# One projection a step in the last head group, and the map combination ahead of the maxima

## What is computed

```python
xn = _layernorm(x, axis=-1)
qkv = xn @ Wqkv_w.T + Wqkv_b                  # 16 query, 8 key heads of 128, values of 4 groups of 256
s = einsum('bqhd,bkhd->bhqk', q, k) * D ** -0.5
p1, p2 = softmax(causal(s)) of the even and of the odd heads
p = p1 - lam * p2
o = einsum('bhqk,bkhe->bqhe', p, v)
o = o * rsqrt(mean(o * o) + EPS) * subln_w * (1.0 - LAMBDA_INIT)
s = o @ out_w.T + out_b
g = silu(quant_dequant_mxfp4(xn) @ quant_dequant_mxfp4(weight).T + bias)
x = x + s * g
```

## Time and profile before

| what | value |
|---|---|
| runs | 1603.66, 1607.04 and 1606.81 us, median 1606.81 us |
| the profiled execution | 1607.1 us |
| its span in the trace | 1605.3 us |
| TensorE busy | 1486.7 us, 93% of the span |
| VectorE busy | 1133.6 us, 71% |
| ScalarE busy | 876.8 us, 55% |
| GpSimd busy | 857.5 us, 53% |

### The profile page before, as it was taken

How to read it: one execution, slowest core, us unless ns; L and a number is a source line. 1 busy time by engine, 2 the same in 40 slices (tenths; PEclk the granted TensorE clock), 3 DMA queues, 4 the chain that set the end, 5 groups by cost and what they waited for, 6 DMA issues and landing times.

```text
span 1605.3 us, 27534 instructions
## 1 busy us (share of the span) xinstructions
PE 1486.7 (93%) x8982; PEld 864.8 (54%) x8982; DVE 1133.6 (71%) x2654; ACT 876.8 (55%) x2474; POOL 857.5 (53%) x1587
## 2 busy tenths in 40 slices
PE   5777879999999989999999999999999998999978
PEld 2444445556555556455565565556564555555644
DVE  5888877667775777757776677757777477775761
ACT  5666765366634666346653566336663466535650
POOL 2566546555465544655455554655546554554543
PEclk9989899999999999999999999999999999999989
DMA  8245453334423453235433335234441344333333
GB/s 262 62 87 132 89 91 65 91 81 74 88 56 89 84 87 76 48 95 84 91 64 91 81 64 96 65 86 83 91 79 43 96 85 90 63 70 76 65 65 73
DMA packets 382496, 134.76 MB, mean 84 GB/s; under 512 B 361872, under 2 KB 365968, under 8 KB 382352
## 3 DMA queue, kind: packets, MB, share of 16 engines
q1 hardware_dynamic: 382352, 132.99, 39.7%
HBM read 35.93 MB, written 8.39 MB: 28 GB/s over the span
## 4 chain that ended last, share of the span: by engine, by line
PE 52%; DVE 16%; ACT 11%; POOL 9%; issue 7%; DMA 4%; SPq 1%; ACTq 0%; POOLq 0%; DVEq 0%
PE ps L544 15%; PE ps L546 14%; PE ps L545 14%; ACT pp L713 4%; DVE ps L1011 3%; DVE qkv L976 3%; PE ps L611 3%; PE ps L613 3%; PE ps L612 3%; ACT ph L722 2%; DMA pT<-ph 2%; ACT qkv L690 2%; DVE ph L1023 2%; POOL qkv L1210 1%; ACT on L735 1%
## 5 line engine op out<-in xcount | busy, mean ns | idle before, releaser
L713 ACT ACTIVATE pp<-ps,row 128x384 f32<-128x384 f32 (+3 forms) x512 | 267.6, 523 | 262.9 <-DVE row L1011 262.7
L1226 POOL TENSOR_TENSOR row<-row,small 128x1 f32<-128x1 f32 x256 | 150.9, 590 | 431.5 <-ACT pp L713 431.5
L544 PE MATMUL ps<-xT,wqkv 128*128 128x512 f16 x768 | 295.6, 385 | 18.8 <-DVE qkv L976 7.8
L1011 DVE CUSTOM_DVE_ANT_0 ps<-ps,mask,ssc 128x384 f32<-128x384 f32 (+3 forms) x512 | 280.0, 552 | 37.5 <-PE ps L613 36.0
L545 PE MATMUL ps<-xT,wqkv 128*128 128x512 f16 x768 | 295.4, 385 | 0.0
L546 PE MATMUL ps<-xT,wqkv 128*128 128x512 f16 x768 | 295.4, 385 | 0.0
L1023 DVE SCALAR_TENSOR_TENSOR ph<-pp,small,ph 128x128 f16<-128x128 f32 (+3 forms) x256 | 152.7, 596 | 128.2 <-ACT ph L722 125.7
L544 PE MATMUL ps<-qkv,pT 128*128 128x256 f16 x640 | 177.6, 277 | 58.0 <-DMA pT<-ph 51.4
L722 ACT ACTIVATE ph<-pp,small 128x128 f16<-128x128 f32 (+3 forms) x256 | 141.4, 553 | 128.3 <-DVE pp L1017 126.5
L976 DVE SCALAR_TENSOR_TENSOR qkv<-ps,bsc,qkv 128x512 f16<-128x512 f32 x192 | 143.2, 748 | 94.0 <-ACT qkv L690 92.9
L544 PE MATMUL ps<-wout,heads 128*128 128x512 f16 x512 | 194.1, 379 | 2.4 <-DVE small L991 1.3
(11 more groups left out here) (132 smaller groups left out, 2977.2 us busy)
## 6 DMA issues: line engine op xcount, KB each, us to landing
xres<-in_x SPq DMA_DIRECT2D x32, 256.0 KB, 3.0
out_x<-res SPq DMA_DIRECT2D x32, 256.0 KB, 2.3
wqkv<-in_wqkv SPq DMA_DIRECT2D x15, 512.0 KB, 6.5
xin<-in_x SPq DMA_DIRECT2D x7, 1024.0 KB, 6.0
vbias<-in_bv SPq DMA_DIRECT2D x32, 128.0 KB, 3.3
pT<-ph SPq DMA_TRANSPOSE x256, 2.7
wout<-in_ow SPq DMA_DIRECT2D x8, 512.0 KB, 4.2
heads<-on SPq DMA_TRANSPOSE x128, 3.2
```

Source lines behind the costliest of these rows:

```text
L544: mm(out, ah, bh, start=start and j == 0, stop=False)
L713: run(out, sc_ps[u][:, m, 0:w], ACT.Exp, bias=ebias[:, u, m:m + 1], scale=-1.0, accum_out=psum_l[:, n % 6, m:m + 1]).then_inc(exp_done, 1)
L1011: nc.vector.tensor_tensor_reduce(sc, sc, mask[:, S - w:S], ssc[:, c:c + 1], BIG, ALU.add, ALU.min, ebias[:, u, m:m + 1]).then_inc(max_done, 1)
```

## The change

Three places are edited. In the list of group 3, the fourth q projection goes from step 19 to step 20, the first v projection from step 20 to 21 and the second from 21 to 22. On VectorE `combine(n+1)` goes ahead of both maxima, in all steps that aren't late. On ScalarE `p_hi(n+1)` goes ahead of the exponentials of map 1.

```diff
@@ schedule
-        at = (None, PROJ_AT, PROJ_AT, (0, 1, 1, 2, 3, 3, 4, 5))[g]
+        at = (None, PROJ_AT, PROJ_AT, (0, 1, 1, 2, 3, 4, 5, 6))[g]
@@ the loop of ScalarE
                 if n and not late:
                     square_o(n - 1)
+                if n + AHEAD - 1 < NSTEPS:
+                    p_hi(n + AHEAD - 1)
                 if n + AHEAD < NSTEPS and not late:
                     exps(n + AHEAD, 1)
-                if n + AHEAD - 1 < NSTEPS:
-                    p_hi(n + AHEAD - 1)
                 if late:
                     square_o(n - 1)
@@ the loop of VectorE
                 late = [f for f in PLAN[n - 1] if f.kind == "out"] if n else []
-                if n + AHEAD < NSTEPS and not late:
-                    maxima(n + AHEAD, 1)
                 if n + AHEAD - 1 < NSTEPS:
                     combine(n + AHEAD - 1)
                 if n + AHEAD < NSTEPS and not late:
+                    maxima(n + AHEAD, 1)
                     maxima(n + AHEAD, 0)
                 if n + AHEAD - 1 < NSTEPS:
                     p_lo(n + AHEAD - 1)
```

## The result

The changed kernel takes 1581.41 us (median of 4 runs, 1578.18 to 1581.99), the kernel before 1605.24 us (median of 4, 1601.55 to 1607.04). The ratio is 0.9847, with a 95% interval of 0.9831 to 0.9863: 1.5% or about 24 us faster. The forecast was 12.3 us, 1595 us, with a range down to 1582, which the median misses by 0.6. The direction was right, the size half of what came.

What follows compares the result with a forecast made beforehand. TensorE was taken to bound the middle batches, VectorE batch 0. Savings of 7.8 (batches 1 to 6), 4.5 (batch 0) and 0 (last batch) make 12.3 us off 1607.1: 1595 us, range 1582 to 1611.

Steps and rivals of the forecast that it cites:

- The list, batches 1 to 6: Moved projections bring the maps of steps 22 and 23 earlier: 1.3 us a batch, 7.8 us over six batches.
- Of these I give 0.6 back: Of 1.9 us a batch won by `attend(23)`, 0.6 returns through gating waits in steps 24, 25 and the transposed input.
- the upper bound: Most the middle batches could win: 5.5 us a batch, all the listed TensorE waits gone.
- The orders in the middle: Both reorderings swap combination for high part in the VectorE-ScalarE ring: taken as 0, within 1.5 us a batch.
- Batch 0: VectorE sets the pace and waits 14.6 us for the map's high part; 4.5 us won, bounds 0 and 14.6.
- is ready in time since two maxima stand between: In batch 0, VectorE no longer waits for the map's high part, 14.6 us in 25 steps before.
- The last batch: FFN tiles hang on VectorE's gating anyway: taken as 0, from a gain of 1.5 to a loss of 3 us.
- `attend(22)` comes some 2 us later: In the last batch, FFN tile and v projection share a bank in step 22, delaying `attend(22)` some 2 us.
- GpSimd falls behind: Rival, chance 0.13: combination meeting GpSimd's norm term costs GpSimd 0.5 us each time; slower, 1613 us.
- More is won: Rival, chance 0.09: maps early in steps 11 to 15 too, batch 0 gives 10 us; about 1579 us.
- The stall only moves: Rival, chance 0.27: new bank, gating, transposition or DMA waits take back the gain of steps 22, 23; 1604 to 1607 us.

Runs made afterwards that it cites:

- Each half alone: Kernel before with one reordering only: VectorE's combination ahead of both maxima, 1662.44 us (1.0358); or ScalarE's high part ahead of the exponential, 1621.75 us (1.0102).
- the orders alone: Kernel before with both reorderings (VectorE's and ScalarE's) and the old list of group 3: 1595.99 us, ratio 0.9943.
- the list alone: Kernel before with only the list of group 3 changed, neither reordering: 1595.55 us, ratio 0.994.

## Why the prediction was right in direction and half in size

**The list, batches 1 to 6: right, and a third too small.** In the four kernels with the new list these batches took 1116.4 to 1119.0 us, in the five executions with the code of before 1126.7 to 1131.4, some 11 us more where the forecast had 7.8. The chain of step 21 came as worked out. VectorE's part of the q fill stands at the end of step 20, `p_lo` of step 21 came earlier, `attend(22)` lost its 1.8 us, the second FFN tile waits for the v projection's sum (4.0 us in four batches, 1.0 each, where the working had 0.9), and the combination waits for the coefficient. The step that failed in size is "Of these I give 0.6 back". In batches 3 to 6 TensorE's waits of steps 22 and 23 fell from 11.3 to 4.0 us, 1.8 us a batch where the working had 1.9, but in steps 24 and 25 they grew from 4.6 to 6.0 only, 0.3 to 0.4 a batch: the gating by 0.3 and the transposed input by 0.5, while 0.4 of the wait with no releaser went away there. The rest of that wait, 2.7 us in step 12, fell to 0.3; I had put it into the upper bound alone. The seven kinds of wait in the view after add up to 15.1 us, against 21.9: 1.7 us a batch. The clock makes single batches differ besides. In batch 2 some 1.5 us more were matmuls at the lower clock in before. In batch 1 some 2 us more were so in the changed kernel, and that batch hardly got shorter, 188.5 us after 188.6.

**The orders in the middle: right at 0.** Each half alone costs 57 and 16 us, and the pair costs nothing that can be told from the scatter of these batches.

**Batch 0: right, a little small.** VectorE's waits for the high part there were 14.6 us, and after:

```profile
DVE ph L1023 <- ACT ph L722: 9.1, 12, 1.6
```

TensorE's waits for maps in batch 0 fell from 24.7 to:

```profile
PE ps L544 <- DMA pT<-ph: 13.5, 5, 3.7
```

Part of that came back as other waits of TensorE in batch 0, for the output's low part above all, 3.5 us before and 8.1 after. Batch 0 got 6.2 us shorter (4.6 with the orders there and nowhere else), the forecast was 4.5, about a third of 14.6. The third was chosen between bounds and not worked out, so its closeness is in part luck. My sentence that the high part "is ready in time since two maxima stand between" held in half of the steps only.

**The last batch: wrong.** "I take 0, from a gain of 1.5 to a loss of 3", for 8.9 us in the profiled executions; the orders there give 2.7 by the medians. I had seen that the FFN tiles hang on the gating and stopped there, instead of following the gating back to the scores, with two instructions of 0.21 and 0.40 us and their hand-overs between that the change takes off that way: 1.1, 1.0 and 0.5 us in three turns, 2.6 together. And I had left the clock out, though the 0.98 of that batch stands in the earlier trace rows beside 1.00. It cost TensorE 5.1 us there in the profiled execution of before and 0.1 in that of the changed kernel; how much of it the change takes away as a rule, and how much is the one execution, isn't settled by the medians. The term also had the list's cost in it, "`attend(22)` comes some 2 us later": the tile of step 22 does wait 1.81 us for the v projection's sum, but the next one then waits 0.94 us for the gating, where it was 2.41.

**The rivals.** *GpSimd falls behind*: the mechanism is there, its price isn't. GpSimd is busy 882.6 us where it was 857.5, and the median of the first instruction of `norm_of` rose from 193 to 442 ns (line 1237 now, 1238 before). It takes over 0.28 us in 145 of its 256 places, against 72, and in most of these the combination runs beside it:

```profile
L1237 POOL TENSOR_TENSOR row<-row x256: 182/442/1170, 63.6 to 1555.5; 128x1 f32<-128x1 f32 x128
```

But ScalarE's wait for it didn't grow against the earlier trace rows:

```profile
ACT on L735 <- POOL row L1239: 82.6, 63, 3.9
```

With the orders alone it is 86.5 us. In the rows above GpSimd's instruction starts at 766.23, VectorE's combination at 766.29, and the first takes 0.86 us while the second takes its usual 0.75. The Trainium skill ("SBUF — State Buffer", Who interferes with whom) has such a pair shut each other out, and the one that is issued first keeps the port. The trace agrees with the exclusion and not with who wins, as far as GpSimd's start can be taken for its issue. *More is won* had the time nearly right, 1579, for a reason that didn't come: TensorE's waits in steps 11 to 15 of batches 3 to 6 fell from 5.7 to 4.5 us only. *The stall only moves* was true of half of it: the map waits of steps 22 and 23, 11.3 us in four batches, are gone, and the waits of steps 22 to 25 together fell by 5.9.

## What to carry to other kernels

Two instructions on two engines that hand over to each other must be moved as a pair: the halves of this reordering lose 57 and 16 us, both together win 10. Before a term is set to nothing because "something else is waited for there", follow that something back as well, and see what the change takes off its way. And a wait of TensorE costs more than its length when the granted clock falls behind it (6.42 us a turn against 4.86 behind the same wait), so the clock column beside a stretch with waits belongs into the sum.

## What was not expected of the hardware

In the 22 us of the last batch in which TensorE waited three times for 2.2 to 2.4 us, the granted clock was 0.77 on average. In the same stretch it was 1.00 with unused matmuls in these waits, and also in the changed kernel, whose waits were 0.9 to 1.8 us. But it isn't the waits alone: with the list alone and waits of 2.44, 1.71, 2.46 and 2.19 us it was 0.92 in the 22 us around them. The same code had more of the lower clock in one execution than in another (5.1 and 3.4 us lost by it), and the length of the last batch went with it, 222.4 and 219.8 us. And in a meeting of VectorE's combination with a GpSimd instruction on one-column operands, the small one paid for all of it: 0.86 us instead of 0.34.
